# Quantisation units per attention quarter: 6, 6, 5, 0 in place of 5 (first two heads) and 4

## The chip, the cores and the metric

One Trainium2 chip, all eight cores of it, one launch. Each core computes half of the tokens of one of four batch rows; the cores exchange nothing. The metric is the device time in microseconds of the slowest core. The median of three runs of the kernel before is 3798.95 us.

## The reference, cut to what matters

```python
xn = _layernorm(x)                                   # x: (4, 4096, 1024) float32
q = xn @ Wq.T                                        # 8 heads of 256
kv = xn @ Wkv_down.T                                 # rank 64
k = kv @ Wk_up.T
v = kv @ Wv_up.T
attn = softmax(einsum('bqhd,bkhd->bhqk', q, k) / 16)
a = einsum('bhqk,bkhd->bqhd', attn, v) @ Wo.T
# fp4(w): blocks of 16 along the last dim, scale = max|w| / 6, rounded to a grid of 8 magnitudes
f = fp4(silu(fp4(xn) @ fp4(w_gate).T) * (fp4(xn) @ fp4(w_up).T)) @ fp4(w_down).T
return x + a + f
```

The gate and up weights are 2816 x 1024, the down weight is 1024 x 2816. Their rounding, fp4(w), depends on nothing but the weights, and it is this work that the change moves.

## The kernel before, in words

The program is five blocks, one after the other, with a barrier between them. Engines have their own instruction lists in each block, in the order in which the Python code emits them, and there is no scheduler.

1. Layer norm of 4096 tokens, their transposes, and the rounding of the core's own 2048.
2. The latent kv and all the queries (`qT_all`), and bounds on the queries' norms.
3. Attention, and beside it the rounding of all three weights. The change is here.
4. Division by the softmax sums, the output projection, the residual.
5. The feed-forward part with the rounded weights.

**Attention.** `for h in range(8)`: first a preparation, then four quarters `qq` of 512 queries. The preparation makes `kT_h` and `V_h` from the latent (PE L633, L642, L645, copied by ACT at L636 and L650), and a bound for the exponent: for each of eight groups of 512 keys ACT squares the keys (L674), PE sums them into one row (L682), and DVE takes the maximum (L692) and merges it (L696 for the first group, L698 for the others). The row of sums goes to one of four PSUM banks, so that from the fifth group on (`grp >= 4`) PE first waits on `pbev`, that is for DVE's maximum of four groups before (the drain at L699). At the end DVE forms the bound (L709, L712), PE spreads it (L717), DVE copies it (L720), and the exponentials can start. A quarter is 32 steps of two score matmuls (L749), one exponential on ACT (L763) and three matmuls with V (L779). After the last, ACT copies the two outputs (L799) and the row of softmax sums (`srowq`, L802), and GpSimd stores this row (`sums<-srowq`), waiting for that copy.

**Rounding.** `emit_wq_units` takes numbered units: 128 rows x 512 columns of a weight (256 columns for every sixth unit of the down weight). NW_UNITS is 44 + 44 + 48 = 136. Of each unit SP issues the load into `wbuf` (two buffers), DVE works through 17 instructions (L212 to L254), and GpSimd issues the store of `wqout` (two buffers). Unit u waits on DVE for its load and for the landing of the store of unit u-2. All DMA streams are issued at L41, so the tile names tell them apart.

**What sets the order.** The units of a quarter are emitted behind the quarter, as in the lines below. DVE has nothing else in a quarter, so it comes to the units early. But GpSimd's list has the store of the quarter's sums row ahead of the stores of the quarter's units. The first two units of a quarter need only the stores of the quarter before; the third waits for the landing of a store that GpSimd issues after the quarter's sums row. Behind the units of the fourth quarter DVE's list goes on with the eight maxima (L692) of the next head.

```python
eb.wait('gpsimd', S['oev'], S['oev'].n)
DS['ssq'].issue(eb, 'gpsimd', sums8[h:h + 1, qq * 512:(qq + 1) * 512], srowq[:, 0, :])
qglob += 1
kq = 5 if qglob <= 8 else 4
emit_wq_units(eb, range(wq_next, wq_next + kq), PL3)
wq_next = min(wq_next + kq, NW_UNITS)
```

From here on heads are counted from 0, and quarters of a head from first to fourth. Before the change heads 0 and 1 have 20 units each and heads 2 to 7 have 16: 40 + 96 = 136.

## Time and profile before

| what | us |
|---|---|
| median of three runs (3796.35, 3798.95, 3927.95) | 3798.95 |
| the profiled execution, its own time | 3800.03 |
| span of its slowest core (core 4); the others 3779.8 to 3795.0 | 3798.4 |
| PE busy in the span | 2556.4 |
| DVE busy in the span | 2458.1 |
| ACT busy in the span | 1244.2 |

The profile is of one execution, on its slowest core. Times in the trace count from the start of the span. "Idle before" names what ended an engine's wait. A matmul's recorded length overlaps that of the next, so PE's busy time is no measure of how fast it goes; the distances between starts are.

### The profile page before, as it was taken

The numbers are of one execution on the slowest core, as the hardware profiler recorded it, in microseconds if no ns is written. First come the engines' busy times: TensorE is split into PE (matmuls) and PEld (weight loads), VectorE is DVE, ScalarE is ACT, GpSimd is POOL, SyncE is SP. The second block draws the span as 40 slices with busy tenths as digits, with TensorE's granted clock in tenths as the row PEclk, the third lists the DMA queues.
The fourth block names the chain that finished last, engine by engine and source line by source line (L and its number), as shares of the span: only waits on it lengthen the run. The fifth ranks groups of instructions, "written<-read, shape, count | busy, mean of one in ns | idle before, by whom it ended". The sixth has DMA issues, their size and how long they took to land. (4 is left out here: it accounts for less than half of the span.)

```text
span 3798.4 us, 36158 instructions; the slowest of 8 cores (3779.8 to 3798.4 us)
## 1 busy us (share of the span) xinstructions
PE 2556.4 (67%) x9848; PEld 953.9 (25%) x9848; DVE 2458.1 (65%) x3881; ACT 1244.2 (33%) x1963; POOL 106.4 (3%) x199
## 2 busy tenths in 40 slices
PE   1111395389597797979899797946955574655756
PEld 1111242022122222222222222212423232222333
DVE  8888703349869585776857485664148768188585
ACT  1111231155455455555555555520012112022121
POOL 0000000000000000000000000000000000000000
PEclk9999997589697897979899797975977786777877
DMA  1111230001101010100101010135340010900202
GB/s 34 33 33 33 89 46 0 7 18 43 32 30 41 22 38 23 37 29 27 38 20 37 19 34 22 32 52 96 133 108 0 28 61 1 171 10 0 89 1 78
DMA packets 126529, 156.29 MB, mean 41 GB/s; under 512 B 77824, under 2 KB 88320, under 8 KB 124288
## 3 DMA queue, kind: packets, MB, share of 16 engines
q1 hardware_dynamic: 41056, 110.25, 9.7%
q10 hardware_dynamic: 69312, 17.31, 3.2%
q0 software_dynamic: 15968, 26.42, 3.0%
q8 instruction: 89, 1.46, 0.2%
q14 instruction: 104, 0.85, 0.1%
HBM read 98.89 MB, written 46.66 MB: 38 GB/s over the span
## 5 line engine op out<-in xcount | busy, mean ns | idle before, releaser
L763 ACT ACTIVATE pbuf<-psA,negB_col 128x512 bf16<-128x512 f32 x512 | 352.0, 688 | 347.1 <-PE psA L749 347.1
L763 ACT ACTIVATE pbuf<-psB,negB_col 128x512 bf16<-128x512 f32 x512 | 351.4, 686 | 284.5 <-PE psB L749 283.6
L779 PE MATMUL psD<-pbuf,V_h 128*128 128x512 bf16 x1024 | 304.5, 379 | 27.5 <-ACT pbuf L763 27.5
L779 PE MATMUL psC<-pbuf,V_h 128*128 128x512 bf16 x1024 | 308.5, 383 | 18.0 <-ACT pbuf L763 18.0
L749 PE MATMUL psA<-qT_all,kT_h 128*128 128x512 bf16 x1024 | 314.9, 390 | 0.4 <-DVEq L721 0.4
L749 PE MATMUL psB<-qT_all,kT_h 128*128 128x512 bf16 x1024 | 313.4, 388 | 0.0
L212 DVE TENSOR_REDUCE pbm<-wbuf 128x32 f32<-128x512 f32 (+1 forms) x136 | 91.1, 670 | 329.2 <-DMA WdqN<-wqout 140.9
L1015 PE MATMUL psC<-hqT_b,wdq_b 128*128 128x512 bf16 x704 | 170.5, 408 | 42.1 <-DVE obuf L1028 38.8
L779 PE MATMUL psE<-pbuf,V_h 128*1 128x512 bf16 x512 | 194.8, 381 | 0.0
L779 PE MATMUL psF<-pbuf,V_h 128*1 128x512 bf16 x512 | 193.0, 377 | 0.0
L342 PE MATMUL psA<-ident_t,xq_f 128*128 128x128 f32 x64 | 17.4, 426 | 241.0 <-DVE xq_f L254 241.0
L1072 PE MATMUL psD<-wgq_b,xqT_sb 128*128 128x512 bf16 (+1 forms) x272 | 108.7, 573 | 72.5 <-DVE h_t L1092 33.8
L978 PE MATMUL psB<-ident_t,hq_t 128*128 128x128 f32 x176 | 45.7, 407 | 157.2 <-DVE hq_t L254 130.7
L1088 ACT ACTIVATE gs_c<-psE 128x512 f32<-128x512 f32 x32 | 19.1, 597 | 386.1 <-DVE h_t L1092 380.4
L978 PE MATMUL psA<-ident_t,hq_t 128*128 128x128 f32 x176 | 45.7, 407 | 141.7 <-DVE hq_t L254 110.2
L779 PEld LDWEIGHTS psD<-pbuf,V_h 128*128 128x128 bf16 x1024 | 97.6, 98 | 153.6 <-issue 40.8
L1028 DVE TENSOR_TENSOR obuf<-rbuf,psC 128x512 f32<-128x512 f32 x64 | 43.4, 686 | 142.2 <-PE psC L1015 101.6
L779 PEld LDWEIGHTS psC<-pbuf,V_h 128*128 128x128 bf16 x1024 | 98.0, 98 | 148.4 <-issue 36.8
L342 PE MATMUL psA<-ident_t,xn_scr 128*128 128x128 f32 x128 | 34.8, 427 | 140.4 <-DVE xn_scr L385 140.4
L1088 ACT ACTIVATE gs_c<-psD 128x512 f32<-128x512 f32 (+1 forms) x34 | 20.1, 591 | 300.1 <-PE psD L1076 175.6
L900 PE MATMUL psC<-o_all,wo_b 128*128 128x512 bf16 x512 | 113.0, 384 | 1.5 <-DVE o_all L882 1.5
L682 PE MATMUL psC<-sqv_t,ones_b 128*1 128x512 bf16 x64 | 32.4, 610 | 118.9 <-ACT sqv_t L674 63.7
(199 smaller groups left out, 4686.0 us busy)
## 6 DMA issues: line engine op xcount, KB each, us to landing
xbuf<-x_tok SPq DMA_DIRECT2D x16, 1024.0 KB, 6.6
rbuf<-resid_scr SPq DMA_DIRECT2D x32, 512.0 KB, 5.5
wbuf<-Wg SPq DMA_DIRECT2D x44, 256.0 KB, 2.8
wbuf<-Wu SPq DMA_DIRECT2D x44, 256.0 KB, 2.8
wbuf<-Wd SPq DMA_DIRECT2D x40, 256.0 KB, 2.7
xt_buf<-xT_own SPq DMA_DIRECT2D x8, 1024.0 KB, 7.0
resid_scr<-rstage SPq DMA_DIRECT2D x8, 1024.0 KB, 4.8
resid_scr<-obuf SPq DMA_DIRECT2D x16, 512.0 KB, 6.0
```

The costliest lines, as they stand in the source:

```text
L212: t_bm = op(lambda e: e.tensor_reduce(out=pbm[:, 0:NB], in_=src3, axis=AX.X, op=ALU.max, apply_absolute_value=True))
L342: ins = (lambda e, c=c, j=j, pbank=pbank, src_tile=src_tile: e.transpose(pbank[:, j * 128:(j + 1) * 128], src_tile[:, c * 128:(c + 1) * 12 ...
L682: ins = (lambda e, pse=pse, m=m: e.matmul(pse[0:1, 0:512], ones_b128[:, 0:1], sqv_t[:, m * 512:(m + 1) * 512], start=(m == 0), stop=(m == 1)))
L749: ins = (lambda e, h=h, qq=qq, kc=kc, m=m, pb=pb: e.matmul(pb[:, :], kT_h[:, m, kc * 128:(kc + 1) * 128], qT_all[:, 2 * h + m, qq * 512:(q ...
L763: eb.em('scalar', lambda e, cglob=cglob, pb=pb: e.activation(out=pbuf[:, cglob % 2, :], in_=pb[:, :], func=AF.Exp, bias=negB_col[:], scale ...
L779: ins = (lambda e, kc=kc, cg=cg, lo=lo, hi=hi, dstp=dstp, dsl=dsl: e.matmul(dstp[dsl, 0:512], V_h[:, kc, lo:hi], pbuf[:, cg % 2, :], start ...
L900: ins = (lambda e, m=m, n=n, kc=kc, pb=pb: e.matmul(pb[:, :], wo_b[:, kc, m * 128:(m + 1) * 128], o_all[:, kc, n * 512:(n + 1) * 512], sta ...
L978: ins = (lambda e, c=c, j=j, pbk=pbk, lg=lg: e.transpose(pbk[:, j * 128:(j + 1) * 128], hq_t[:, lg % 2, c * 128:(c + 1) * 128], ident_t[:]))
L1015: ins = (lambda e, m=m, n2=n2, it=it, pb=pb: e.matmul(pb[:, :], wdq_b[:, it, m * 128:(m + 1) * 128], hqT_b[:, it, n2 * 512:(n2 + 1) * 512] ...
L1028: eb.em('vector', lambda e, m=m, n2=n2, pb=pb: e.tensor_tensor(out=obuf[:, m % 2, n2 * 512:(n2 + 1) * 512], in0=rbuf[:, m % 2, n2 * 512:(n ...
L1072: eb.em('tensor', lambda e, tt=tt, c0=c0, clen=clen, kc2=kc2, pg=pg, toff=toff: e.matmul(pg[:, 0:clen], xqT_sb[:, kc2, toff + tt * 128:tof ...
L1088: eb.em('scalar', lambda e, clen=clen, pg=pg: e.activation(out=gs_c[:, 0:clen], in_=pg[:, 0:clen], func=AF.Silu).then_inc(S['sil'].h, 1))
```

## The change

One line is changed. The number of units behind a quarter now depends on the quarter alone: six, six, five and none.

```diff
@@ -804,7 +804,7 @@
             eb.wait('gpsimd', S['oev'], S['oev'].n)
             DS['ssq'].issue(eb, 'gpsimd', sums8[h:h + 1, qq * 512:(qq + 1) * 512], srowq[:, 0, :])
             qglob += 1
-            kq = 5 if qglob <= 8 else 4
+            kq = [6, 6, 5, 0][(qglob - 1) % 4]
             emit_wq_units(eb, range(wq_next, wq_next + kq), PL3)
             wq_next = min(wq_next + kq, NW_UNITS)
```

Each head now has 17 units, 8 x 17 = 136. The units themselves, their order, the lists of PE, ACT and SP, and the number of instructions are as they were. What moves is where the heads' other instructions stand among the units on DVE, and where the sums rows stand among the stores on GpSimd.

DVE, the end of head 0 and the first maxima of head 1 (lines with a minus stand there only before). L212 to L254 are the 17 instructions of one unit:

```order
-L239 SCALAR_TENSOR_TENSOR PL3pD<-PL3pA,PL3pD 128x512
-L241 SCALAR_TENSOR_TENSOR PL3pC<-PL3pA,PL3pC 128x512
-L244 SCALAR_TENSOR_TENSOR PL3pC<-PL3pC,PL3pD 128x512
-L250 TENSOR_TENSOR PL3pC<-PL3pC,PL3pK 128x512
-L254 TENSOR_TENSOR wqout<-PL3pC,pscale 128x512
 L692 TENSOR_REDUCE bt<-psC 1x1
 L696 TENSOR_SCALAR bt<-bt 1x1
```

The piece with a minus is 51 instructions long, three units; they now stand behind the maxima of head 1. At the end of head 1 six units have moved so (40 before, 34 now).

GpSimd, head 2, from its first sums row to the loads of a later head's weights (`wkuh`, `wvuh`). Before:

```order
L41 DMA sums<-srowq 1x16x32
L41 DMA WgqN<-wqout 128x512 x4
L41 DMA sums<-srowq 1x16x32
L41 DMA WuqN<-wqout 128x512 x4
L41 DMA sums<-srowq 1x16x32
L41 DMA WuqN<-wqout 128x512 x4
L41 DMA sums<-srowq 1x16x32
L41 DMA WuqN<-wqout 128x512 x4
L41 DMA wkuh<-WkuT 64x256
```

and now:

```order
L41 DMA sums<-srowq 1x16x32
L41 DMA WgqN<-wqout 128x512 x6
L41 DMA sums<-srowq 1x16x32
L41 DMA WgqN<-wqout 128x512 x4
L41 DMA WuqN<-wqout 128x512 x2
L41 DMA sums<-srowq 1x16x32
L41 DMA WuqN<-wqout 128x512 x5
L41 DMA sums<-srowq 1x16x32
L41 DMA wkuh<-WkuT 64x256
```

All 17 stores of the head now stand ahead of its fourth sums row.

GpSimd, the end of the block (L819 is the branch at its end, after the barrier's signal). Before:

```order
L41 DMA sums<-srowq 1x16x32
L41 DMA WdqN<-wqout 128x512 x3
L41 DMA WdqN<-wqout 128x256
L819 UNCONDITIONAL_BRANCH
```

and now:

```order
L41 DMA WdqN<-wqout 128x512 x4
L41 DMA WdqN<-wqout 128x256
L41 DMA sums<-srowq 1x16x32
L819 UNCONDITIONAL_BRANCH
```

The last thing that GpSimd issues in the block is now a sums row, and no unit is emitted behind the last quarter.

Of the kernel before, what the change touches and what calls it, by code (L numbers as in the profile page):

```python
# [82 lines left out]
def build_program(debug=False, stop_after=9):  # L83
# [186 lines left out]
    def emit_wq_units(eb, us, PL):  # L270
        for u in us:
            if u >= NW_UNITS:
                continue
            src, dst, F = wq_units[u]
            if u >= 2:
                eb.wait('sync', S['wqd'], u - 1)
            DS['win'].issue(eb, 'sync', wbuf[:, u % 2, 0:F], src)
            DS['win'].wait_for(eb, 'vector', u)
            if u >= 2:
                DS['wqs'].wait_for(eb, 'vector', u - 2)  # L280
            last = emit_quant(eb, F, wbuf[:, u % 2, 0:F], wqout[:, u % 2, 0:F], PL)
            S['wqd'].n += 1
            eb.em('vector', lambda e, last=last: last(e).then_inc(S['wqd'].h, 1))
            eb.wait('gpsimd', S['wqd'], S['wqd'].n)
            DS['wqs'].issue(eb, 'gpsimd', dst, wqout[:, u % 2, 0:F])
# [315 lines left out]
    qglob = 0  # L601
    cglob = 0
    kt0_dump_tgt = [0]
    for h in range(NH):
# [131 lines left out]
        for qq in range(4):  # L736
            par = qq % 2
            o0, o1, osum = OAB[par]
            exp_tgt = [0] * 32

            def emit_scores(kc):
                nonlocal cglob
                pb = SBK[cglob % 2]
                if cglob >= 2:
                    eb.wait('tensor', S['exp'], cglob - 1)
                if h == 0 and qq == 0 and kc == 0:
                    eb.wait('tensor', S['pbev'], S['pbev'].n)
                for m in range(2):
                    ins = (lambda e, h=h, qq=qq, kc=kc, m=m, pb=pb: e.matmul(  # L749
                        pb[:, :], kT_h[:, m, kc * 128:(kc + 1) * 128],  # L750
                        qT_all[:, 2 * h + m, qq * 512:(qq + 1) * 512],
                        start=(m == 0), stop=(m == 1)))
                    if m == 1:
                        S['sco'].n += 1
                        eb.em('tensor', lambda e, ins=ins: ins(e).then_inc(S['sco'].h, 1))
                    else:
                        eb.em('tensor', ins)
                eb.wait('scalar', S['sco'], S['sco'].n)
                if qq == 0 and kc == 0:
                    eb.wait('scalar', S['bnd'], bnd_ready)  # L760
                S['exp'].n += 1
                exp_tgt[kc] = S['exp'].n
                eb.em('scalar', lambda e, cglob=cglob, pb=pb: e.activation(  # L763
                    out=pbuf[:, cglob % 2, :], in_=pb[:, :], func=AF.Exp,
                    bias=negB_col[:], scale=SCALE).then_inc(S['exp'].h, 1))
                cglob += 1

            def emit_av(kc, cg):
                eb.wait('tensor', S['exp'], exp_tgt[kc])
                if kc == 0 and qglob >= 2:  # L770
                    eb.wait('tensor', S['oev'], qglob - 1)
                if kc == 0 and qq == 0:
                    eb.wait('tensor', S['pbev'], pbev_ready)
                for mt2 in range(3):
                    lo = [0, 128, 256][mt2]
                    hi = [128, 256, 257][mt2]
                    dstp = [o0, o1, osum][mt2]
                    dsl = (slice(0, 128), slice(0, 128), slice(0, 1))[mt2]
                    ins = (lambda e, kc=kc, cg=cg, lo=lo, hi=hi, dstp=dstp, dsl=dsl: e.matmul(  # L779
                        dstp[dsl, 0:512], V_h[:, kc, lo:hi], pbuf[:, cg % 2, :],  # L780
                        start=(kc == 0), stop=(kc == 31)))
                    if mt2 == 2 and kc == 31:
                        S['avq'].n += 1
                        eb.em('tensor', lambda e, ins=ins: ins(e).then_inc(S['avq'].h, 1))
                    else:
                        eb.em('tensor', ins)

            cg0 = cglob
            for kc in range(32):
                emit_scores(kc)  # L790
                if kc >= 1:
                    emit_av(kc - 1, cg0 + kc - 1)
            emit_av(31, cg0 + 31)
            eb.wait('scalar', S['avq'], S['avq'].n)
            if qglob >= 1:
                DS['ssq'].wait_for(eb, 'scalar', qglob - 1)
            for m in range(2):
                op = [o0, o1][m]
                eb.em('scalar', lambda e, h=h, qq=qq, m=m, op=op: e.copy(  # L799
                    o_all[:, 2 * h + m, qq * 512:(qq + 1) * 512], op[:, :]))  # L800
            S['oev'].n += 1
            eb.em('scalar', lambda e, qglob=qglob, osum=osum: e.copy(  # L802
                srowq[:, 0, :], osum[0:1, 0:512]).then_inc(S['oev'].h, 1))
            eb.wait('gpsimd', S['oev'], S['oev'].n)
            DS['ssq'].issue(eb, 'gpsimd', sums8[h:h + 1, qq * 512:(qq + 1) * 512], srowq[:, 0, :])
            qglob += 1
            kq = 5 if qglob <= 8 else 4
            emit_wq_units(eb, range(wq_next, wq_next + kq), PL3)
            wq_next = min(wq_next + kq, NW_UNITS)

# [366 lines left out]
```

## Rows read from the trace of the kernel before

**Rows 1.** Waits of PE from 732 to 2540 us (attention): total, times, longest
```profile
PE psC L682 <- ACT sqv_t L674: 63.7, 30, 2.7
PE psC L682 <- DVEq L699: 55.2, 2, 27.8
```

**Rows 2.** Timeline of PE: the fifth group's sum (L682) of heads 1 and 3
```profile
1006.39 1.01 PE L682 MATMUL psC<-sqv_t,ones_b 128*1 128x512 bf16 x2 [27.39 <-DVEq L699]
...
1462.88 1.01 PE L682 MATMUL psC<-sqv_t,ones_b 128*1 128x512 bf16 x2 [1.93 <-ACT sqv_t L674]
```

**Rows 3.** Timeline of ACT: the last copy of the fourth quarter, heads 0 to 3 and 7
```profile
953.78 0.57 ACT L802 COPY srowq<-psF 1x512 f32<-1x512 f32 x1
1194.32 0.57 ACT L802 COPY srowq<-psF 1x512 f32<-1x512 f32 x1
1435.73 0.57 ACT L802 COPY srowq<-psF 1x512 f32<-1x512 f32 x1
1651.20 0.57 ACT L802 COPY srowq<-psF 1x512 f32<-1x512 f32 x1
...
2511.54 0.57 ACT L802 COPY srowq<-psF 1x512 f32<-1x512 f32 x1
```

**Rows 4.** Timeline of POOL (GpSimd): issues in heads 0, 1, 2, 3 and 7
```profile
826.58 0.51 POOL L41 DMA_DIRECT2D sums<-srowq  x1 [50.55 <-ACT srowq L802]
...
839.61 0.54 POOL L41 DMA_DIRECT2D WgqN<-wqout  x1 [11.31 <-DVE wqout L254]
...
957.53 0.72 POOL L41 DMA_DIRECT2D sums<-srowq  x1
...
976.55 0.54 POOL L41 DMA_DIRECT2D WgqN<-wqout  x1 [9.21 <-DVE wqout L254]
...
1005.86 0.54 POOL L41 DMA_DIRECT2D WgqN<-wqout  x1 [9.23 <-DVE wqout L254]
...
1066.90 0.50 POOL L41 DMA_DIRECT2D sums<-srowq  x1 [49.07 <-ACT srowq L802]
...
1217.16 0.54 POOL L41 DMA_DIRECT2D WgqN<-wqout  x1 [9.21 <-DVE wqout L254]
...
1308.50 0.50 POOL L41 DMA_DIRECT2D sums<-srowq  x1 [49.71 <-ACT srowq L802]
...
1459.87 0.54 POOL L41 DMA_DIRECT2D WuqN<-wqout  x1 [9.23 <-DVE wqout L254]
...
1523.79 0.50 POOL L41 DMA_DIRECT2D sums<-srowq  x1 [49.46 <-ACT srowq L802]
...
1538.07 0.54 POOL L41 DMA_DIRECT2D WuqN<-wqout  x1 [12.62 <-DVE wqout L254]
...
2384.29 0.51 POOL L41 DMA_DIRECT2D sums<-srowq  x1 [63.25 <-ACT srowq L802]
...
2397.21 0.61 POOL L41 DMA_DIRECT2D WdqN<-wqout  x1 [11.32 <-DVE wqout L254]
2403.42 0.54 POOL L41 DMA_DIRECT2D WdqN<-wqout  x1 [5.60 <-DVE wqout L254]
...
2512.68 0.51 POOL L41 DMA_DIRECT2D sums<-srowq  x1 [19.57 <-ACT srowq L802]
...
2532.17 0.54 POOL L41 DMA_DIRECT2D WdqN<-wqout  x1 [5.95 <-DVE wqout L254]
2540.47 1.18 POOL L843 DMA_DIRECT2D wo_b<-WoT  x1 [7.76 <-POOLq L819]
```

**Rows 5.** Timeline of DVE: the first wait in head 0, the first maximum of head 3
```profile
829.37 0.69 DVE L212 TENSOR_REDUCE pbm<-wbuf 128x32 f32<-128x512 f32 x1 [29.45 <-DMA WgqN<-wqout]
...
1459.23 0.67 DVE L692 TENSOR_REDUCE bt<-psC 1x1 f32<-1x512 f32 x1
1459.97 0.14 DVE L696 TENSOR_SCALAR bt<-bt 1x1 f32<-1x1 f32 x1
```

**Rows 6.** Windows (busy PE, PEld, DVE, ACT, POOL; clock, DMA, GB/s): two preparations, one quarter
```profile
955.00:1022.00 67.00, 23.00 (x67) 6.01 (x66) 53.41 (x106) 24.86 (x48) 5.05 (x9) 0.51 0.11 37
1437.00:1479.00 42.00, 23.59 (x68) 6.24 (x66) 25.26 (x53) 24.81 (x48) 3.63 (x7) 0.51 0.11 33
...
869.00:912.00 43.00, 41.16 (x160) 12.31 (x160) 39.33 (x78) 23.42 (x36) 3.23 (x6) 1.00 0.15 47
```

**Rows 7.** Timeline of DVE: the first instruction of block 4
```profile
2540.08 12.94 DVE L857 RECIPROCAL sums<-sums 8x2048 f32<-8x2048 f32 x1 [8.47 <-PEq L819]
```

## The prediction

> **What bounds the kernel now.** I read the waits of PE over the attention block first, because the change touches nothing outside it. In [rows 1] the wait to look at is the one on DVE's drain L699: 55.2 us in two waits, the longest 27.8. All other waits in L682 are short ones for ACT's squares, a fixed part of every preparation (at most 2.7 us each). Next I read the timeline around the longer ones. [rows 2] has the same instruction at two head boundaries, both times the fifth group of the preparation: in head 1 PE had waited 27.39 us for DVE, in head 3 only 1.93 us for ACT. So at this boundary the attention block stands still for DVE, and at the other it does not.
>
> What that costs is read from the ends of heads [rows 3]. From the fourth quarter of head 0 to that of head 1 is 1194.32 - 953.78 = 240.54 us, then 241.41, and then 215.47 us to the end of head 3, with the same work on PE and ACT. The windows [rows 6] say where: 67 us of preparation ahead of head 1, 42 us ahead of head 3, with the same PE and ACT work in both, and DVE busy 53 us rather than 25. In a quarter PE has 41 us of records in 43 and sets the pace; DVE is beside it.
>
> Why DVE is late is read from GpSimd's issues [rows 4], which mark the end of each unit. In head 0 the third unit's store is at 839.61 and the twentieth's at 1005.86: 17 steps in 166.25 us, 9.78 us each, with no pause. A quarter is (2512.68 - 2384.29) / 3 = 42.8 us by the distance of the first and the fourth sums row of head 7, so DVE can do 4.4 units a quarter, and heads 0 and 1 ask five. Before that run DVE sat idle 29.45 us for the landing of a store [rows 5], which GpSimd could not issue before the first sums row. That is the gate: at most two units run ahead of the end of a quarter. In heads 2 to 7, with four units a quarter, the gate stops DVE in every quarter, and the last two units of the fourth run in the preparation.
>
> **The change part by part.** I call the first sums row's issue S, and count a head's units 1 to 17 (20 or 16 before).
>
> *Boundaries after heads 0 and 1.* The limit for DVE: in head 3's preparation PE starts the fifth sum 1462.88 - 1435.73 = 27.15 us after ACT's last copy [rows 2, 3]. That puts the limit at 953.78 + 27.15 = 980.93 in head 1 and at 1221.47 in head 2. DVE's first maximum releases PE about 0.3 us after the last store's issue (the store of the last unit of head 2 is issued at 1459.87, L696 runs at 1459.97 and ends at 1460.1 [rows 4, 5]). The run of units in head 0 is already the one that the change leaves, cut by three at the end. Unit 17 is stored at 976.55 and in head 1 at 1217.16 [rows 4], 150.0 and 150.3 us after S. Released at 976.9 and 1217.5, PE would find the maximum done 4.0 us early at both. So both waits shrink to the 1.93 us for ACT: 27.39 - 1.93 = 25.5 and 27.8 - 1.93 = 25.9, together 51.4 us. The ends of heads give the same from another side: 240.54 + 241.41 - 2 x 215.47 = 51.0. I take 51.3.
>
> *Boundaries after heads 2 to 6.* Here the change adds a unit, 16 to 17. It is not paid, because the gates go. Now the gate holds once a head: the third unit waits for S, and after it 15 units run on, since unit 9, the next gated one, comes to its turn at S + 13.0 + 5 x 9.77 = S + 61.9, long after the second sums row at S + 42.8. Unit 17 ends at S + 150.1, where S + 128.4 is the fourth sums row, which GpSimd issues 1.1 us after ACT's copy starts (2512.68 against 2511.54 [rows 3, 4]). The limit is then S + 128.4 - 1.1 + 27.15 = S + 154.4, and DVE is there 4.0 us early. Head 3 had the slowest landing, 14.28 us from S to the third store against 13.03 in head 0 [rows 4]; with that the margin is 2.7. In heads 5 and 6 two and three of the 17 units are short ones, 6.21 us (2397.21 to 2403.42 [rows 4]), and the margin is over 10 us. I take nothing for these five boundaries. The ends: at best nothing too, since PE is not held there today; at worst the unit added is paid whole, 9.8 - 4.0 = 5.8 us in three boundaries (after heads 2, 3 and 4), 17 us.
>
> *What the longer run queues behind it.* ACT waits at the end of a quarter for the landing of the sums row before. The third row now stands behind unit 12's store on GpSimd, S + 13.0 + 9 x 9.77 = S + 101, and is needed at S + 127; the fourth behind unit 17's, S + 150, and is needed a whole preparation and a quarter later. Cost nothing; if that cover were gone the end of each quarter would wait. SP's loads stay one unit ahead as before.
>
> *The end of the block.* Before, the last store is issued 2532.17 - 2512.68 = 19.5 us after the last sums row is ready. Now head 7 has 14 units after the third, three of them short: 12.9 + 11 x 9.77 + 3 x 6.21 = 139.0, so S + 139.0, which is 10.6 us behind the end of the quarter, and the sums row follows it at once, 0.5 us. Gain 19.5 - 10.6 - 0.5 = 8.4 us. Block 4 begins 2540.08 - 2532.17 = 7.9 us after GpSimd's last issue [rows 4, 7]; the trace does not say what of these 7.9 us is the landing of that store and what the barrier. I keep them. The bounds for the end of the block are 0 (something else holds the barrier) and 19.5 (the quarter's end alone would hold it); I take 8.4.
>
> *Clock.* The preparation is at a granted clock of 0.51, with the stall and without it [rows 6], and the quarter is at 1.00, so a shorter pause gives PE nothing more and takes nothing.
>
> *Sum.* 51.3 + 8.4 = 59.7 us. Blocks 4 and 5 only start earlier. The profiled execution took 3800.03, so 3740.3; it lies 1.1 us above the median of the runs shown, so 3739 us is what I expect of a median, 1.6% less.
>
> A rule of the Trainium skill speaks against it. [rows 4] first: GpSimd's issue of a sums row takes 0.50 us when DVE waits, and 0.72 us at 957.53 in the middle of a dense run; the unit pitch in that run is 9.78 us as elsewhere. "GPSIMD Engine Reference", section 8 "Key points", says that GpSimd shares its SBUF interfaces with VectorE, with contention against DVE instructions in a two-port mode or with two SBUF inputs, which most of a unit's are. By that rule more issues fall into dense DVE work than before and both could slow; the trace agrees for the issue alone, at 0.2 us.
>
> **The rivals.** A measurement of this kernel can tell about 2%, 76 us, from no change.
>
> *The added unit is paid (3756).* For it: 17 units where 16 just fit today, and a margin of 2.7 to 4 us in a run of 150. Against it: heads 0 and 1 show that very run on the same engine at 9.78 us. Price as above, 17 us: 3739 + 17 = 3756, and a little under that for a part of it.
>
> *The end of the block stays (3747).* For it: the 7.9 us are unexplained, and the store of the sums row is now last. Against it: DVE's last unit must end before the barrier, and it ends earlier. Time 3739 + 8.4 = 3747.
>
> *Slower: the dense run stretches (3830).* One mechanism: units slow down when 15 of them follow each other beside the stores in every head, and DVE then comes late at seven boundaries instead of two. The limit leaves (154.4 - 0.3 - 13.0) / 14 = 10.1 us a unit. At 11 us a unit DVE is 14 x 1.23 - 4.0 = 13.2 us late after heads 0 to 4, 6 and 3 us after heads 5 and 6, in all 75 us; it saves the 51.3 us and loses about 16 of the end of the block: -51.3 + 75 + 16 - 8.4 = +31 us, so 3830. It becomes slower than before at about 10.7 us a unit. Against it: 9.78 us over 17 steps in a row.
>
> *It does not do what it says.* The counts must end at 136 with none behind the last quarter; they do (8 x 17), so I give this no weight.
>
> **How the numbers follow.** The forecast of 3739 gets 0.78, the paid unit 0.09, the end that stays 0.08, slower 0.03, and 0.02 for a larger gain, if the ends of blocks 4 and 5 shift in favour. The forecast's own spread is 8 us either way: 3 us between the runs shown, the 4 us between my two readings of the 51 and the end, and blocks 4 and 5, whose clock alternates. The range reaches up through both milder rivals and a little past them: 3729 to 3763. Faster by over 2% would need 76 us, 16 more than every term here gives: 0.04. Slower by over 2% is at the far end of the last rival: 0.01. The rest is within 2%.
>
> **What would show it.** In the profile of the changed kernel: PE's waits have no row for L682 on DVE's L699 above a few us; all eight heads are 215 us apart; the stores from the third unit of a head on are 9.8 us apart, and unit 17's is at S + 150; DVE waits for a store's landing once a head, not up to four times; block 4 begins about 60 us earlier than 2540, near 2480. The prediction is wrong if a row of PE for L699 stays at several boundaries, or if the heads shorten and the time does not.

## The result and the profile after

The changed kernel took 3736.18 us in its profiled execution, against 3800.03. The ratio to the kernel before is 0.9847 with a 95% interval of 0.9818 to 0.9876, which on the 3799 us of before is 58 us less (47 to 69); 3739 was forecast, 60 less. The gain of 1.5% is less than the 2% that the prediction wanted in order to tell a change from none, but its interval is clear of 1. The ratios leave out executions, and the table below leaves out cores, in which a die ran at a clearly lower granted clock; the plain medians of ten, 3752.16 and 3801.95, hold such executions and are not compared.

The waits of PE in the attention block of the changed kernel (total, times, longest), to be held against [rows 1]:

```profile
PE psC L682 <- ACT sqv_t L674: 67.6, 32, 2.7
PE psD L682 <- ACT sqv_t L674: 61.7, 32, 1.9
PE psD L779 <- ACT pbuf L763: 27.5, 32, 1.5
```

The row of 55.2 us for DVE's L699 is gone, and only ACT's fixed wait has come in its place: ACT's row has two more waits (32 for 30) and 3.9 us more, the 2 x 1.93 us that were to be left. The ends of heads on ACT, as in [rows 3], for the first four heads and the last:

```profile
951.93 0.57 ACT L802 COPY srowq<-psF 1x512 f32<-1x512 f32 x1
1167.43 0.57 ACT L802 COPY srowq<-psF 1x512 f32<-1x512 f32 x1
1382.51 0.57 ACT L802 COPY srowq<-psF 1x512 f32<-1x512 f32 x1
1597.75 0.57 ACT L802 COPY srowq<-psF 1x512 f32<-1x512 f32 x1
...
2458.03 0.57 ACT L802 COPY srowq<-psF 1x512 f32<-1x512 f32 x1
```

The heads are 215.5, 215.1 and 215.2 us apart where they were 240.5, 241.4 and 215.5. GpSimd's issues, to be held against [rows 4]: the first sums row and unit 17 of head 0, the same of head 3, then the end of the block:

```profile
824.72 0.52 POOL L41 DMA_DIRECT2D sums<-srowq  x1 [50.03 <-ACT srowq L802]
...
974.71 0.54 POOL L41 DMA_DIRECT2D WgqN<-wqout  x1 [9.24 <-DVE wqout L254]
975.24 0.51 POOL L41 DMA_DIRECT2D sums<-srowq  x1
...
1470.33 0.50 POOL L41 DMA_DIRECT2D sums<-srowq  x1 [49.25 <-ACT srowq L802]
...
1621.98 0.55 POOL L41 DMA_DIRECT2D WuqN<-wqout  x1 [9.23 <-DVE wqout L254]
...
2470.24 0.54 POOL L41 DMA_DIRECT2D WdqN<-wqout  x1 [5.97 <-DVE wqout L254]
2470.77 0.51 POOL L41 DMA_DIRECT2D sums<-srowq  x1
2479.36 1.21 POOL L843 DMA_DIRECT2D wo_b<-WoT  x1 [8.09 <-POOLq L819]
```

Unit 17 comes 149.99 us after the first sums row in head 0 and 151.65 in head 3. How near that is to the limit shows in head 3's preparation, on PE and DVE, the tightest of the five full heads:

```profile
1621.34 0.67 DVE L692 TENSOR_REDUCE bt<-psC 1x1 f32<-1x512 f32 x1
...
1624.89 1.01 PE L682 MATMUL psC<-sqv_t,ones_b 128*1 128x512 bf16 x2 [1.93 <-ACT sqv_t L674]
```

DVE's first maximum begins at 1621.34 and is merged and drained some 0.9 us later; PE starts the fifth sum at 1624.89, held by ACT alone. The margin is 2.6 us. DVE's own waits for stores show the other half of the mechanism, one gate a head (eight waits) where there were 26:

```profile
DVE pbm L212 <- DMA WuqN<-wqout: 85.3, 3, 29.5
DVE pbm L212 <- DMA WgqN<-wqout: 85.2, 3, 28.9
DVE pbm L212 <- DMA WdqN<-wqout: 55.7, 2, 27.9
```

For all kernels below I use three stretches of each core: from GpSimd's memset of V_h (L588, the start of the attention block) to ACT's last copy (L802); from there to DVE's first instruction of block 4 (L857); and from there to the end of the span. They are worked out from those three rows of each core.

| kernel | attention, us | last copy to block 4, us | rest, us |
|---|---|---|---|
| before | 1777.7 to 1779.4 | 28.5 to 28.6 | 1245 to 1258 |
| changed | 1723.9 to 1727.9 | 20.9 to 21.0 | 1246 to 1256 |
| e1_even | 1724.3 to 1727.0 | 28.8 to 28.9 | 1239 to 1255 |
| e2_end | 1777.8 to 1779.2 | 10.7 to 10.9 | 1246 to 1259 |
| e3_eighteen | 1758.2 to 1761.5 | 9.0 | 1247 to 1265 |
| e4_late (cores 4 to 7) | 1839.9 to 1842.8 | 48.4 | 1248 to 1257 |
| e5_gate | 1723.8 to 1726.4 | 9.0 to 9.1 | 1240 to 1255 |
| e6_gate_new | 1724.9 to 1727.4 | 9.3 to 9.4 | 1240 to 1260 |
| e7_seven | 1723.4 to 1724.9 | 9.3 to 9.4 | 1241 to 1250 |

The means of the cores are 1778.6 and 1725.8 us for the attention of the two kernels: 52.8 us less there, 7.6 less at the end of the block, and the rest unchanged within its own scatter.

### The profile page after: what moved, and what is told of

The parts are those of the page before. It is cut to its first block and busy times, and to the rows that moved or that the text cites. A ratio compares the mean times of both kernels' runs of the same rounds, so it can differ in the third digit from the quotient of the medians.

```text
span 3734.5 us, 36158 instructions; the slowest of 8 cores (3719.4 to 3734.5 us)
## 1 busy us (share of the span) xinstructions
PE 2550.7 (68%) x9848; PEld 952.9 (26%) x9848; DVE 2458.8 (66%) x3881; ACT 1244.1 (33%) x1963; POOL 108.3 (3%) x199
## 5 line engine op out<-in xcount | busy, mean ns | idle before, releaser
L212 DVE TENSOR_REDUCE pbm<-wbuf 128x32 f32<-128x512 f32 (+1 forms) x136 | 91.2, 670 | 240.9 <-DMA WuqN<-wqout 85.3
L1015 PE MATMUL psC<-hqT_b,wdq_b 128*128 128x512 bf16 x704 | 168.4, 404 | 46.1 <-DVE obuf L1028 42.8
L244 DVE SCALAR_TENSOR_TENSOR PL3pC<-PL3pC,PL3pD 128x512 f32<-128x512 f32 (+1 forms) x136 | 92.0, 677 | 24.6 <-DVE PL3pC L241 24.6
```

The lines of the kernel that those rows point to most:

```text
L212: t_bm = op(lambda e: e.tensor_reduce(out=pbm[:, 0:NB], in_=src3, axis=AX.X, op=ALU.max, apply_absolute_value=True))
L244: t_q = op(lambda e: e.scalar_tensor_tensor(out=pC[:, 0:F], in0=pC[:, 0:F], scalar=0.5, in1=pD[:, 0:F], op0=ALU.mult, op1=ALU.add))
L1015: ins = (lambda e, m=m, n2=n2, it=it, pb=pb: e.matmul(pb[:, :], wdq_b[:, it, m * 128:(m + 1) * 128], hqT_b[:, it, n2 * 512:(n2 + 1) * 512] ...
```

## The experiments

**e1_even and e2_end: the two terms apart.**

```diff
-            kq = 5 if qglob <= 8 else 4
+            kq = [5, 4, 4, 4][(qglob - 1) % 4]
```

> 17 units in every head, but as 5, 4, 4, 4 over the quarters: the number per head of the changed kernel, without its empty fourth quarter. Theory A (the gain is DVE's lateness at the boundaries after heads 0 and 1, 51 us, and a shorter end of the block, 8 us): units 16 and 17 run behind the fourth sums row as in heads 2 to 7 before, so no boundary is late, and the end stays as before: 51 us under the kernel before, ratio 0.9865, 8 us above the changed kernel; all heads 215 us apart. Rival B (the empty fourth quarter makes the gain): no or little gain, two or more boundaries late. Rival C (only the number per head counts): the time of the changed kernel, ratio 0.985 or lower, block 4 as early as there.

Measured: ratio 0.9866 (0.9848 to 0.9884). No wait on L699; attention as short as in the changed kernel, the end of the block as long as before. GpSimd's issues at the end of the block:

```profile
2462.44 0.51 POOL L41 DMA_DIRECT2D sums<-srowq  x1 [19.55 <-ACT srowq L802]
2462.95 1.10 POOL L41 DMA_DIRECT2D WdqN<-wqout  x2
2475.38 0.61 POOL L41 DMA_DIRECT2D WdqN<-wqout  x1 [11.32 <-DVE wqout L254]
2481.93 0.54 POOL L41 DMA_DIRECT2D WdqN<-wqout  x1 [5.95 <-DVE wqout L254]
2490.55 1.18 POOL L843 DMA_DIRECT2D wo_b<-WoT  x1 [8.09 <-POOLq L819]
```

The last store is 19.5 us behind the last sums row, as in the kernel before. So the empty fourth quarter is not what frees the boundaries; taking three units from each of the first two heads is. Rival B falls, and rival C for the end of the block.

```diff
-            kq = 5 if qglob <= 8 else 4
+            kq = 5 if qglob <= 8 else 4 if qglob <= 28 else [6, 6, 4, 0][(qglob - 1) % 4]
```

> Counts of before in heads 0 to 6 (5 a quarter, then 4), and in head 7 its 16 units as 6, 6, 4, 0. Theory A: the waits after heads 0 and 1 stay at 27 us, and the last store comes 129.2 us after the head's first sums row, 0.8 us behind the last quarter, where it was 19.5 behind: block 4 begins 18 us earlier, ratio 0.9952. Rival B (the end of the block makes most of the changed kernel's gain): 40 to 60 us, ratio 0.985 to 0.990. Rival D (the 7.9 us from the last issue to block 4 are the landing, or something other than DVE holds the barrier): 0 to 10 us.

Measured: ratio 0.9952 (0.9934 to 0.9970), attention unchanged, 10.8 us from the last copy to block 4, 17.8 less. PE's wait at both boundaries is there as before; its total in the waits of PE:

```profile
PE psC L682 <- DVEq L699: 55.4, 2, 27.9
```

The two edits add up from separate places, and both landed on the forecast: 51 and 18 us less than before.

**e3_eighteen and e4_late: is there a limit, and where.**

```diff
-            kq = 5 if qglob <= 8 else 4
+            kq = [6, 6, 6, 0][(qglob - 1) % 4] if qglob <= 28 else [5, 5, 0, 0][(qglob - 1) % 4]
```

> One unit more than the changed kernel in heads 0 to 6 (6, 6, 6, 0), ten in head 7 (5, 5, 0, 0). Theory A with its limit of 154.4 us after the first sums row: unit 18 releases PE at 160.2, 5.8 us late, at the five boundaries whose heads have only full units (after heads 0 to 4), and in time after heads 5 and 6 with their short ones; the end of the block is held by the quarter alone and is 19.5 us shorter than before. Sum against before: -51.3 + 29 - 19.5 = -42 us, ratio 0.989; PE's waits on L699 show five of 5 to 8 us. Rival E (there is no such limit, PE is not held by a unit more): five boundaries free, -71 us, ratio 0.981. Rival F (the limit is nearer): over 10 us at each boundary, ratio over 0.994.

Measured: ratio 0.9907 (0.9886 to 0.9929). The timeline of PE has five waits on L699, at the first five boundaries; the first and the fourth of them, and their total in the waits:

```profile
985.67 1.01 PE L682 MATMUL psC<-sqv_t,ones_b 128*1 128x512 bf16 x2 [7.91 <-DVEq L699]
...
1652.35 1.01 PE L682 MATMUL psC<-sqv_t,ones_b 128*1 128x512 bf16 x2 [8.94 <-DVEq L699]
```

```profile
PE psC L682 <- DVEq L699: 42.0, 5, 8.9
```

Less the 1.93 us that ACT would take anyway in each, that is 32 us for 29 forecast, 6.0 to 7.0 us each for 5.8; the boundaries after heads 5 and 6 are free. One unit more than the change has is one too many in a head without short units, so the margin of 2.7 to 4 us was real. In the whole the kernel gained some 35 us, not 42: 3 us of the difference are these waits, the rest lies in blocks 4 and 5, within their scatter.

```diff
-            kq = 5 if qglob <= 8 else 4
+            kq = [3, 4, 4, 6][(qglob - 1) % 4]
```

> 17 units in every head, but as 3, 4, 4, 6: most of them in the fourth quarter. Theory A: four units run behind the fourth sums row, the last is stored 42.2 us after it, and PE is 16.5 us late after heads 0 to 4 and 13 us after heads 5 and 6, 108 us in all; the end of the block is 19.5 us longer. Against before -51.3 + 108 + 19.5 = +76 us, ratio 1.020, seven waits on L699. Rival C (only the number per head counts): the time of the changed kernel, ratio 0.985.

Measured: ratio 1.0232 (1.0187 to 1.0277), slower than before. The waits of PE:

```profile
PE psC L682 <- DVEq L699: 126.2, 7, 19.9
```

Seven waits; this row is core 0's, and the same row on cores 4 to 7 is 127.0 to 128.4 us. After taking off 7 x 1.93 that is 113 to 115 us, for 108 forecast; the end of the block is 19.9 us longer for 19.5. Attention grew by 63 us on cores 4 to 7, for 57 forecast. The ratio still holds the profiled execution, 3906.43 us. The other two in it, 3876.33 and 3879.72 us, are 77 and 80 us above 3799.69, for 76 forecast. With the same 17 units in each head, the placement alone makes 3.7% between this kernel and the changed one (1.0207, by those two executions only, against 0.9847). Rival C is gone.

**e5_gate, e6_gate_new: the gate.** The store of the sums row is moved behind the stores of the quarter's units; e5_gate keeps the counts of before, e6_gate_new has those of the change.

```diff
-            eb.wait('gpsimd', S['oev'], S['oev'].n)
-            DS['ssq'].issue(eb, 'gpsimd', sums8[h:h + 1, qq * 512:(qq + 1) * 512], srowq[:, 0, :])
             qglob += 1
             kq = 5 if qglob <= 8 else 4
             emit_wq_units(eb, range(wq_next, wq_next + kq), PL3)
             wq_next = min(wq_next + kq, NW_UNITS)
+            eb.wait('gpsimd', S['oev'], S['oev'].n)
+            DS['ssq'].issue(eb, 'gpsimd', sums8[h:h + 1, qq * 512:(qq + 1) * 512], srowq[:, 0, :])
```

> Counts of before (5 a quarter in heads 0 and 1, then 4), but GpSimd stores a quarter's sums row behind the stores of the quarter's units, not ahead of them, so that units are held back by the quarter before and not by their own. Theory A (heads 0 and 1 were late because the gate leaves DVE idle for 29 us in their first quarter, not because 20 units are too many for a head): DVE starts 44.6 us before the first sums row and runs 20 units without a pause, 195.5 us, to 151 us after it, 3 us inside the limit of 154.4; no wait on L699 although 20 units stand before the boundary. The end of the block is then held by the last quarter, 19.5 us earlier. Sum -51.3 - 19.5 = -71 us, ratio 0.9814, 11 us under the changed kernel. Rival G (20 units a head are too many, whatever the gate): two waits of about 25 us stay, ratio 0.995. Rival H (dense DVE work from the start of the first quarter on slows ACT, PE or the unit): quarters longer than 42.8 us or units longer than 9.8 us, ratio over 0.985.

Measured: ratio 0.9762 (0.9712 to 0.9811), an interval that ends just below the 0.9814 forecast, and 0.9784 (0.9738 to 0.9831) in the second comparison below, which holds it. No wait on L699 but for one of 1.9 us on core 7, the length of ACT's own, although head 0 has 20 units ahead of the boundary as before. GpSimd's issues in head 0, the first unit and the twentieth:

```profile
787.85 0.60 POOL L41 DMA_DIRECT2D WgqN<-wqout  x1 [14.72 <-DVE wqout L254]
...
973.69 0.54 POOL L41 DMA_DIRECT2D WgqN<-wqout  x1 [9.24 <-DVE wqout L254]
```

19 steps in 185.84 us, 9.78 us each, without a pause. The twentieth stands 152.5 us after ACT's first copy of the sums (821.2 here). In [rows 4] it stands 180.5 us after that copy (1005.86 against 825.4), so it is 28 us earlier in its head; another 4 us between the two times come from the earlier start of this core. So 20 units were never too many for a head; they were late because DVE lay idle for 29 us behind the gate at the head's start. Rival G falls. The quarters are 42.8 us as ever and the unit pitch too, so rival H falls as well.

> The counts of the change (6, 6, 5, 0) with the sums row behind the units. Theory A: DVE ends a head's 17 units 121.6 us after the first sums row, before the last quarter ends; nothing of the attention block waits for DVE, and the end is held by PE and ACT. The same floor as the counts of before with this order: -71 us, ratio 0.9814; the counts no longer matter. Rival C (the counts have a value of their own): clearly lower than the kernel with the counts of before and this order.

Measured: ratio 0.9777 (0.9735 to 0.9818). With the gate moved, the counts of before and of the change give the same attention within 2 us and the same end of the block within 0.4 us. In these kernels the value of the counts lies only in how they meet the gate.

**e7_seven: the counts alone.**

```diff
-            kq = 5 if qglob <= 8 else 4
+            kq = ([6, 6, 5, 0] if h < 5 else [6, 6, 6, 0] if h < 7 else [6, 6, 3, 0])[qq]
```

> The gate as before, the counts 6, 6, 5, 0 in heads 0 to 4, 6, 6, 6, 0 in heads 5 and 6, and 6, 6, 3, 0 in head 7 (85 + 36 + 15 = 136). Theory A: head 5 with two short units of 18 releases PE at 153.1 to 153.7 us after its first sums row, just inside 154.4, head 6 with three at 149.5; no boundary late by more than 1 us, and head 7's 15 units end 119.5 us after its first sums row, before the quarter ends, so that the block's end is held by the quarter: 10.6 us under the changed kernel, ratio 0.9815. Rival I (what remains of the changed kernel's end is the barrier, not DVE's last units): the time of the changed kernel, 0.984.

Measured: 3717.18 us in the profile, and a ratio of 0.9791 (0.9735 to 0.9847) in the second comparison below. No wait on L699. Head 5's boundary on core 2, DVE's first maximum and PE's fifth sum:

```profile
2051.49 0.67 DVE L692 TENSOR_REDUCE bt<-psC 1x1 f32<-1x512 f32 x1
...
2053.22 1.01 PE L682 MATMUL psC<-sqv_t,ones_b 128*1 128x512 bf16 x2 [1.93 <-ACT sqv_t L674]
```

DVE is done less than a microsecond before PE would have waited for it. The end of the block is held by the quarter alone: 9.3 us.

**The three versions on one chip.** The changed kernel had been run again on the chip of e5 to e7:

> The changed kernel again, on the chip of the three below, as their comparison: ratio 0.984 to 0.986 (59 us under the kernel before), no wait of PE on L699, block 4 60 us earlier.

Its profiled execution took 3739.68 us; no ratio came of this run. A second comparison of three of the kernels followed.

> The changed kernel once more, as the comparison of the two below on one chip: ratio 0.9845 +- 0.002.

> Counts of before, sums row behind the units. Theory A: attention block as short as in the changed kernel and its end 12 us shorter (9.0 us from ACT's last copy to block 4, against 20.9), so 12 us under the changed kernel on the same chip, ratio to the kernel before 0.981 to 0.982. The single look (20 us under the changed kernel's two) owed its other 8 us to blocks 4 and 5, which the edit does not touch; if they are a gain of the edit, the ratio is 0.979 or lower again.

> Counts 17, 17, 17, 17, 17, 18, 18, 15, gate as before. Theory A: the same as the kernel above within 2 us (9.3 us from ACT's last copy to block 4), ratio 0.981 to 0.982; the counts alone can reach the floor, and so can the order alone.

Measured against the kernel before on this chip: the changed kernel 0.9815 (0.9769 to 0.9861), the moved gate 0.9784 (0.9738 to 0.9831), the counts of e7_seven 0.9791 (0.9735 to 0.9847). The first ratio lies below my band of 0.9845 +- 0.002, though 0.9845 is inside its interval; the other two lie below the forecast of 0.981 to 0.982 by 0.002 to 0.003. The part common to all three is the kernel before. Of its eight executions in these ratios five lie between 3795 and 3799 us, and three are at 3810, 3821 and 3843. Against the median of the five, 3798.3, the three kernels are at 0.984, 0.981 and 0.980, within 0.001 of the forecasts. The first comparison, that of e5 and e6, likewise has three longer executions of the kernel before among six (3815 to 3822 us); against the other three the medians of e5_gate and e6_gate_new are at 0.980 and 0.981.

The medians of the five executions that each ratio holds are 3738.6, 3726.3 and 3723.7 us: the two versions are 12 and 15 us faster than the changed kernel, for 12 forecast, though the intervals of the ratios overlap. Of the 20 us of the first comparison 12 were the end of the block. By the means of the cores in the two profiles attention differs by 1.7 us and blocks 4 and 5 by 3, and in the two profiles of the same moved-gate kernel blocks 4 and 5 differ by 12 (1248 and 1260 us), so nothing shows a further gain of the edit. Both versions beat the two kernels of this study, one by the order on GpSimd, one by counts alone.

## Why the prediction was right

*The two boundaries.* Forecast 51.3 us, measured 52.8 on the means of eight cores; the wait itself fell by 55.2 - 2 x 1.93 = 51.3, and the other 1.5 are less than the cores differ among themselves. The step that carried it, reading head 0's own run of units cut at the seventeenth as what the changed kernel would do, held to 0.1 us: 149.99 us after the first sums row for 149.97. e1_even shows the term alone.

*The boundaries after heads 2 to 6.* Forecast nothing, measured nothing, with a margin in head 3 of 2.6 us for the 2.7 worked out. The agreement to 0.1 us is in part luck: the third unit was stored 0.5 us later than assumed (14.80 us after the first sums row for 14.28), and a head without pauses and a limit 0.15 us further off took most of that back. e3_eighteen put a price on the next unit, 6.0 to 7.0 us a boundary for 5.8. The excess is the slower landing in head 3 (14.36 us for 13.0) and, in heads 1, 2 and 4, the pauses of 0.36 us between units that occur now and then in all kernels; I left them out of the 9.77. This also shows a flaw in the first rival. Its 9.8 - 4.0 us was called the price of the seventeenth unit, but the margin of 4.0 us had already counted that unit; it is the price of an eighteenth, and nothing in the rows gave the seventeenth 17 us.

*The end of the block.* Forecast 8.4, measured 7.6. The last unit came 11.1 us behind the quarter for 10.6, and block 4 began 8.2 us after the last issue for 7.9. The first part is the last short unit: its store comes 6.57 us after the one before it (2470.24 against 2463.67), where I took 6.21; the 5.95 us of waiting in the last unit's line of [rows 4], for 5.60 in that of an earlier short one, had said so. The term was mis-sized by 0.8 us. e2_end shows it alone. Its upper bound, 19.5 us, is what e5_gate collects, and e7_seven to within 0.3.

*The clock.* Forecast no effect. In the windows of the changed kernel the preparation of head 1 has a granted clock of 0.52, about the lower of the two levels, and a quarter 1.00, the upper, as in [rows 6]:

```profile
953.00:995.00 42.00, 23.58 (x68) 6.22 (x66) 26.66 (x56) 24.89 (x48) 3.17 (x6) 0.52 0.10 30
867.00:910.00 43.00, 41.16 (x160) 12.29 (x160) 39.33 (x78) 23.44 (x36) 3.43 (x6) 1.00 0.14 47
```

*The rivals.* The paid unit and the unmoved end did not come. The stretched run did not either: the pitch in head 0 of the changed kernel is (974.71 - 837.74) / 14 = 9.78 us. The prediction read from one row that GpSimd's issue of a sums row is slower in a dense run. More rows say otherwise. In the kernel before, the sums rows at 869.25 and 912.12, in the same dense run as the 0.72 us at 957.53, took 0.51 us. In the changed kernel 13 of the 32 sums rows took 0.67 to 0.72 us, and in each of them DVE's TENSOR_SCALAR of L215 (0.42 us long, where its two-input instructions take 0.69) began 0.16 to 0.21 us after the issue did; beside the two-input L233 and L235, at 2373.57, the issue took 0.51. The Trainium skill ("GPSIMD Engine Reference", section 8, "Key points") names both kinds of DVE instruction, a two-port mode and two SBUF inputs, as sources of contention over the shared SBUF interfaces. The trace shows nothing for the second kind at these issues; that L215 is of the first kind is not shown, and no run here isolates the cause. The unit pitch stayed at 9.78 us, and the time does not feel it.

## What to carry to other kernels

Work on an engine that is "off the path" is bounded by where its in-order list meets the path: read the distance between the last filler instruction and the first one that another engine waits for, at every boundary, and put a number on the margin. A wait on another queue (here a store behind a store that waits for the quarter's end) can cost such an engine more than its load; look for the idle time before you reduce the work. Even counts were enough for most of the gain; the rest lay in the end of the block, where the last filler must end before the last useful work does.

## What I had not expected

The time from GpSimd's last issue to block 4 does not depend on what that issue stores. In e3_eighteen the last store of a weight was issued at 2439.78, long before, and the last issue was a row of 512 numbers:

```profile
2439.78 0.54 POOL L41 DMA_DIRECT2D WdqN<-wqout  x1 [5.97 <-DVE wqout L254]
2450.72 0.51 POOL L41 DMA_DIRECT2D sums<-srowq  x1 [10.40 <-ACT srowq L802]
2493.51 0.49 POOL L41 DMA_DIRECT2D sums<-srowq  x1 [42.29 <-ACT srowq L802]
2501.76 1.21 POOL L843 DMA_DIRECT2D wo_b<-WoT  x1 [7.75 <-POOLq L819]
```

GpSimd still waits 7.75 us between the two, as it did for 7.76 in [rows 4]. The trace also says where the time goes. GpSimd's DRAIN at the block's end (L819) stands at 2500.9, 6.9 us after that issue ended, and its first issue in the new block comes 0.9 us later; in the kernel before, the DRAIN is at 2539.6, again 6.9 us after the issue. ACT's and DVE's DRAINs stand at 2493.1 and 2439.4, so the barrier waits for GpSimd's. The profile's median from issue to landing is 2.1 us for a sums row, so the landing by itself is too short to explain the 6.9 us; what GpSimd does in them stays open. The wait has two values: 7.75 to 7.76 us in the kernel before, e2_end, e3_eighteen and e5_gate, and 8.08 to 8.09 us in the changed kernel, e1_even, e4_late, e6_gate_new and e7_seven, on all eight cores of each. The 0.3 us by which block 4 came later than forecast are this difference; its cause was not tried.

Blocks 4 and 5 vary from 1239 to 1270 us between cores that run the same instructions (all profiles but cores 0 to 3 of e4_late, which reach 1281), whatever was edited ahead of them. A single execution cannot show a gain below some 10 us in the whole time, while within one kernel, with the same cores left out, the stretches of the attention block repeat within some 4 us, and its end within 0.3.
